# Cross-attention over the top ten rows: the first query projection in 32-column tiles, four side by side, in place of 64-column pairs

## The chip, the cores and the metric

The kernel runs on one core of one Trainium2 chip. The metric is the device time of one execution in microseconds (us). The kernel before took 146.26 us, the median of three runs (146.04 to 146.67). Instructions, waits and transfers are read from one profiled execution, taken by the hardware profiler.

## The reference

There are 8 batches. `x` is 8 x 224 x 512, the context is 8 x 750 x 512, all float32. For each batch:

```
scores   = x @ score_w + score_b                    # one number per row of x
topk_idx = top_k(scores, 10)
sparse   = x[topk_idx]                              # 10 rows of 512
q = sparse @ Wq.T + bq      (16 heads of 32)
k = ctx @ Wk.T + bk ;  v = ctx @ Wv.T + bv
attn = softmax(q k^T / sqrt(32))                    # 16 heads, 10 x 750
out  = (attn @ v) @ out_w.T + out_b
x[topk_idx] = out                                   # the other rows of x are returned as they came
```

The biases are eight times those first drawn. The output is all of `x` with ten rows per batch replaced.

## The kernel before, in words

Five engines run programs of their own, written out by hand, and wait for each other on semaphores. TensorE (PE) takes its matmuls in the order of the program at L762 to L794; nothing is reordered around a wait. The batches are worked in two groups: group 0 is batches 0 and 1, group 1 is batches 2 to 7 (`GROUPS`, L33). Group 0 is started as early as possible, so that TensorE has attention work while the rest of `x` is still arriving and being scored.

**The start, group 0.** SyncE (L191 to L200) queues, with no waits in between, two batches of `x`, Wq, one batch of `x`, Wk, two batches of `x`, the context columns of batch 0, the last three batches of `x`, the columns of batch 1 and the context rows of batches 0 and 1. A batch of `x` is 512 KB in memory. VectorE (DVE) scores each batch as it lands (two `tensor_tensor_reduce` per batch, L350), finds the top ten rows of group 0 (L366 to L378), and TensorE picks and transposes these 20 rows with small matmuls (`pick_rows` L590, `join_rows` L600) into `picked_T[0]`, which ScalarE copies out of PSUM (L275). `keep_warm` (L561) fills some of TensorE's waits with matmuls that nobody reads.

**The query projection, `project_queries(g)` (L620 to L635).** It computes Wq times the picked rows. The 512 outputs are four blocks `e` of 128, the 512 inputs four blocks `t` of 128. For each `e` and `t` the 128 outputs are cut into tiles of `TILE` = 64 columns of weights; the two tiles write to PSUM partitions 0 to 63 and 64 to 127, so they lie side by side in the array. Group 0 has 20 columns of moving data (2 batches x 10 rows), group 1 has 60. Each group has 4 x 4 x 2 = 32 calls. Each float32 call shows in the trace as two weight loads and two matmul records, so a group has 64 of each. Blocks `e` = 0 and 1 are the first half and end with one increment of `q_ps`, blocks 2 and 3 the second half with another.

**What takes the queries.** `spread_queries` on VectorE (L399 to L413) waits for each half, adds the bias (L405), spreads the result by head (L409) and increments `q_done`. VectorE has score work ahead of it and behind it: after both halves come the second product of batch 3, batch 4, a maximum over the key-bias terms (`copy_key_dot`, L434, which waits for four ScalarE copies at L297), and then batches 5, 6 and 7 (L527 to L532). `fold_keys` on TensorE (L637 to L650) waits for `q_done` 1, multiplies the first half by the key weights for all four steps, waits for `q_done` 2 and does the second half: 64 records each way, 80 columns wide. Then come `dot_key_bias(0)` (L677), in four tiles of 32 columns, and the logits of batch 0, `logits_by_step` (L700), 24 calls per batch and 48 records.

**The meeting point.** Ahead of the 21st of those 24 calls stands `transpose_scores(1)` (L575, placed by L778). It waits until VectorE has scored all eight batches and added the score bias (L363), and gives VectorE the scores of group 1 to choose from. TensorE takes nothing behind it before that. Four calls of batch 0 follow, then eight of batch 1 up to `move_idx` (L608). VectorE then chooses the rows of group 1, and turns to the softmax of batches 0 and 1.

**Afterwards** the batches follow each other: logits (L700, L714), softmax on VectorE and ScalarE, weighted sums of the context (`weigh`, L731). `project_queries(1)` lies inside the weighing of batch 1 (L782). SyncE loads further context when the logits of an earlier batch are done (L203 on). At the end come the value projection (`project_values`, L746, 32-column tiles, four side by side, 80 columns of moving data), the output projection (L758), and a scatter of 80 rows by GpSimd (L259).

Of the kernel before, what the change touches and what calls it, by code (L numbers as in the profile page):

```python
# [22 lines left out]
HEADS, TOPK = 16, 10  # L23
DH = D // HEADS
P = 128
# [19 lines left out]
FIRST = GROUPS[0][1]  # L45
PART = 32
TILE = 64
EARLY_COPIES = 5


def build(nc, x, x_lines, ctx_rows, ctx_cols, wq, wk, wv, wo, in_bias, out_b, score_row, out):
# [5 lines left out]
    with stack:  # L57
        def sb(name, shape, dt=F32):
            return stack.enter_context(nc.sbuf_tensor(name, shape, dt))
# [9 lines left out]
        wq_sb = sb("wq_sb", [P, DT, D])  # L69
# [31 lines left out]
        picked_T = [sb(f"picked_T{g}", [P, DT, b1 * TOPK]) for g, (b0, b1) in enumerate(GROUPS)]  # L101
# [35 lines left out]
        query_ps = [[logits_ps[1][:, 0, :], logits_ps[1][:, 1, :]], [logits_ps[0][:, 1, :], logits_ps[0][:, 0, :]]]  # L137
# [34 lines left out]
        def _(sp):  # L172
# [8 lines left out]
            def load_rows(b, n):  # L181
                sp.dma_start(ctx_r[n][:, :, :], ctx_rows[b, :, :, :]).then_inc(ctx_r_in[n], 16)
# [5 lines left out]
            def copy_x(b):  # L188
                sp.dma_start(out_pairs[:, b, :, :], x_sb[0:X_P, b, :, :]).then_inc(x_copied, 16)
# [22 lines left out]
            sp.dma_start(wo_sb[:, :, :], wo).then_inc(wo_in, 16)  # L212
            for b in range(EARLY_COPIES):
                copy_x(b)
            sp.wait_ge(logits_done, 3)
            load_cols(4, 0)
            for b in range(5, B):
# [3 lines left out]
                load_rows(b - 1, (b - 1) % 2)  # L221
                copy_x(EARLY_COPIES + b - 5)
            sp.wait_ge(mix_ready[1], B - 2)
# [334 lines left out]
        def _(pe):  # L558
# [36 lines left out]
            def join_rows():  # L595
                pe.wait_ge(regroup_done, 2 * FIRST + 1)
                pe.wait_ge(parts_done, 2)
                for t in range(DT):
                    for j in range(P // TILE):
                        last = nc.tensor.matmul(picked_ps[0][j * TILE:(j + 1) * TILE, t * FIRST * TOPK:(t + 1) * FIRST * TOPK],  # L600
                                                parts[:, t * P + j * TILE:t * P + (j + 1) * TILE],
                                                regroup[:, :, :].rearrange("p b q -> p (b q)"), start=True, stop=True)
# [17 lines left out]
            def project_queries(g):  # L620
                b0, b1 = GROUPS[g]
                nq = (b1 - b0) * TOPK
                if g:
                    pe.wait_ge(idx_ready, 1)
                pe.wait_ge(picked_T_done, g + 1)
                for half in range(2):
                    for k in range(2):
                        e = 2 * half + k
                        for t in range(DT):
                            for j in range(P // TILE):  # L630
                                c = e * P + j * TILE
                                last = nc.tensor.matmul(query_ps[g][half][j * TILE:(j + 1) * TILE, k * nq:(k + 1) * nq],  # L632
                                                        wq_sb[:, t, c:c + TILE], picked_T[g][:, t, b0 * TOPK:b1 * TOPK],
                                                        start=(t == 0), stop=(t == DT - 1), skip_group_check=True)
                    last.then_inc(q_ps, 1)  # L635

# [135 lines left out]
            join_rows()  # L772
            pe.wait_ge(wq_in, 16)
            project_queries(0)
            pe.wait_ge(wk_in, 16)
            fold_keys()
# [3 lines left out]
            logits_by_step(1, 1, [], {8: move_idx})  # L780
            weigh(0, 0, {})
            weigh(1, 1, {12: transpose_picked, 18: lambda: project_queries(1)})  # L782
            fold_pairs()
            dot_key_bias(1)
# [48 lines left out]
```

## Time and profile before

| what | value |
|---|---|
| median of three runs | 146.26 us (146.04 to 146.67) |
| the profiled execution, its own device time | 146.49 us |
| its span in the profile, first to last record | 144.3 us |
| TensorE (PE) busy | 136.3 us, 94% |
| TensorE weight loads (PEld) busy | 127.3 us, 88% |
| VectorE (DVE) busy | 81.8 us, 57% |
| first query projection, L632, group 0 | starts at 14.13 us, 64 records |
| `transpose_scores(1)`, L575 | starts at 25.64 us |

2.19 us of the device time lie outside the span. Times of single instructions are taken from the span's start. "PE" rows are matmuls, whose ends are modelled, so their durations overlap; the distance from one start to the next tells how fast they go. That distance is worked out from a merged row: (length of the row - mean duration of one) / (count - 1). "Idle before" in brackets is how long the engine had been idle ahead of a row, and for what.

### The profile page before, as it was taken

The page shows a single profiled execution, that of the slowest core. Times are in us where ns is not written, and L with a number is a line of the kernel's source. Part 1 is how long each engine was busy: PE and PEld are TensorE (multiplying, and loading weights), DVE is VectorE, ACT ScalarE, POOL GpSimd, SP SyncE. Part 2 cuts the span into 40 slices and gives each one's busy share as a digit, 9 for nine tenths or more (in the row PEclk, how much of TensorE's full clock was granted, in tenths as well). Part 3 has the DMA queues.
Part 4 walks back from the last instruction along what each step waited for, and adds up shares of the span by engine and source line. Part 5 has one row for each costly group of instructions (what it writes and reads, how often), then busy time and mean ns, then how long its engine had stood idle before and what let it go on. Part 6 is the DMA issues. An engine that isn't in the chain of part 4 may idle for free.

```text
span 144.3 us, 2951 instructions
## 1 busy us (share of the span) xinstructions
PE 136.3 (94%) x1262; PEld 127.3 (88%) x1262; DVE 81.8 (57%) x214; ACT 23.1 (16%) x48; POOL 4.7 (3%) x24
## 2 busy tenths in 40 slices
PE   7997997899999999999999999999999999999980
PEld 5544996898999998999999999999999999998840
DVE  2977658887880559088871575087138506735330
ACT  3001050003412051003140041005002300411100
POOL 6000000030000000000000000000000000000002
PEclk9999999999999999999999999999999999999997
DMA  4999999999988079999989884995880390000001
GB/s 157 395 409 418 422 409 360 433 429 379 407 269 371 7 252 420 326 395 398 427 320 313 297 356 119 343 302 235 269 294 0 49 392 0 0 5 0 5 0 45
DMA packets 5726, 37.61 MB, mean 261 GB/s; under 512 B 801, under 2 KB 801, under 8 KB 3410
## 3 DMA queue, kind: packets, MB, share of 16 engines
q1 hardware_dynamic: 5344, 36.93, 67.6%
q0 software_dynamic: 128, 0.33, 0.7%
q8 instruction: 10, 0.16, 0.5%
q10 hardware_dynamic: 242, 0.17, 0.5%
q14 instruction: 2, 0.02, 0.0%
HBM read 33.60 MB, written 3.83 MB: 259 GB/s over the span
## 4 chain that ended last, share of the span: by engine, by line
PE 76%; DMA 12%; SPq 4%; DVE 3%; issue 1%; POOLq 1%; ACT 1%; DVEq 0%
PE mix_ps L731 37%; PE logits_ps L714 23%; DMA x_sb<-x_lines_dram 12%; PE logits_ps L700 7%; PE logits_ps L758 3%; SPq L186 2%; PE logits_ps L666 2%; PE logits_ps L632 1%; PE mix_ps L666 1%; DVE product L350 1%; PE misc_ps L746 1%; ACT probs L306 1%; POOLq L57 1%; PE logits_ps L746 1%; SPq L179 1%
## 5 line engine op out<-in xcount | busy, mean ns | idle before, releaser
L731 PE MATMUL mix_ps<-probs,ctx_r 125*128 125x160 f32 x384 | 54.0, 300 | 0.2 <-ACT probs L306 0.2
L731 PEld LDWEIGHTS mix_ps<-probs,ctx_r 125*128 125x128 f32 x384 | 52.5, 190 | 1.0 <-issue 0.9
L714 PE MATMUL logits_ps<-qk,ctx_c 128*125 128x160 f32 x240 | 33.4, 299 | 0.0
L714 PEld LDWEIGHTS logits_ps<-qk,ctx_c 128*125 128x125 f32 x240 | 32.9, 188 | 0.0
L444 DVE TENSOR_REDUCE col_max<-logits_ps 125x160 f32<-125x960 f32 x8 | 9.2, 1154 | 25.7 <-PE logits_ps L714 21.3
L700 PE MATMUL logits_ps<-qk,ctx_c 128*125 128x160 f32 x144 | 20.5, 301 | 0.0
L700 PEld LDWEIGHTS logits_ps<-qk,ctx_c 128*125 128x125 f32 x144 | 19.6, 188 | 0.5 <-issue 0.4
L310 ACT ACTIVATE mix<-mix_ps 128x320 f32<-128x320 f32 x16 | 7.0, 440 | 64.5 <-PE mix_ps L731 64.4
L482 DVE TENSOR_REDUCE prob_sum<-probs 125x160 f32<-125x960 f32 x8 | 14.6, 1836 | 4.0 <-ACT probs L306 4.0
L306 ACT ACTIVATE probs<-probs 125x480 f32<-125x480 f32 x16 | 9.3, 603 | 29.3 <-DVE probs L476 29.3
L350 DVE CUSTOM_DVE_ANT_0 product<-x_sb,score_w_sb 112x512 f32<-112x512 f32 x16 | 10.4, 688 | 1.1 <-DMA x_sb<-x_lines_dram 1.1
L476 DVE TENSOR_TENSOR probs<-logits_ps,shift 125x480 f32<-125x480 f32 x16 | 9.8, 652 | 0.3
L561 PE MATMUL logits_ps<-ones 128*128 128x256 f32 (+2 forms) x16 | 7.6, 615 | 1.1 <-DVE ones L507 1.1
L561 PEld LDWEIGHTS logits_ps<-ones 128*128 128x128 f32 x16 | 4.1, 284 | 3.8 <-issue 2.5
L259 POOL DMA_INDIRECT out_dram<-y_sb,row_idx x1 | 0.9, 922 | 110.1 <-DVE y_sb L504 110.1
L632 PE MATMUL logits_ps<-picked_T,wq_sb 128*64 128x20 f32 (+1 forms) x128 | 4.1, 218 | 0.4 <-ACT picked_T L275 0.4
L632 PEld LDWEIGHTS logits_ps<-picked_T,wq_sb 128*64 128x64 f32 x128 | 3.9, 138 | 0.7 <-issue 0.7
L466 DVE COPY head_shift<-head_shift 32x5 f32<-32x5 f32 x24 | 3.9, 163 | 0.8
L405 DVE TENSOR_TENSOR q_sb<-logits_ps,bias_sb 128x40 f32<-128x40 f32 (+1 forms) x4 | 1.0, 240 | 5.9 <-PE logits_ps L632 5.9
L454 DVE COPY quad_max<-quad_max 32x5 f32<-32x5 f32 x24 | 3.8, 160 | 0.8
L487 DVE RECIPROCAL inv_sum<-misc_ps 128x320 f32<-128x320 f32 x1 | 2.2, 2158 | 3.5 <-PE misc_ps L684 3.5
L758 PE MATMUL logits_ps<-wo_sb,o_T 128*80 128x256 f32 x16 | 3.7, 381 | 0.0
(97 smaller groups left out, 75.2 us busy)
## 6 DMA issues: line engine op xcount, KB each, us to landing
ctx_r<-ctx_rows_dram SPq DMA_DIRECT2D x8, 1536.0 KB, 7.0
ctx_c<-ctx_cols_dram SPq DMA_DIRECT2D x6, 1500.0 KB, 9.0
x_sb<-x_lines_dram SPq DMA_DIRECT2D x8, 512.0 KB, 10.9
out_dram<-x_sb SPq DMA_DIRECT2D x8, 448.0 KB, 12.4
ctx_c<-ctx_cols_dram SPq DMA_DIRECT2D x4, 750.0 KB, 16.5
wq_sb<-wq_dram SPq DMA_DIRECT2D x1, 1024.0 KB, 7.0
wk_sb<-wk_dram SPq DMA_DIRECT2D x1, 1024.0 KB, 9.8
wv_sb<-wv_dram SPq DMA_DIRECT2D x1, 1024.0 KB, 9.6
```

What stands on the lines that cost most here:

```text
L306: nc.scalar.activation(part, part, ACT.Exp, scale=SCALE).then_inc(exp_done, 1)
L310: nc.scalar.activation(mix[:, 2 * half:2 * half + 2, :, b * TOPK:(b + 1) * TOPK], mix_ps[half][:, 0:2 * HQ].rearrange("p (t h q) -> p t h ...
L350: nc.vector.tensor_tensor_reduce(out=products[j][:, :], in0=x_sb[0:X_P, b, j, :], in1=score_w_sb[:, :], scale=1.0, scalar=0.0, op0=ALU.mul ...
L444: nc.vector.tensor_reduce(col_max[0:S_P, :], tiles(n).rearrange("p k t c -> p c k t"), AX.XY, ALU.max)\
L476: nc.vector.tensor_tensor(probs[n][:, k * BANK_T:(k + 1) * BANK_T, :], tiles(n)[:, k, :, :], shift[0:S_P, :].unsqueeze(1).broadcast_to([S_ ...
L482: nc.vector.tensor_reduce(prob_sum[:, b, :], probs[n][:, :, :].rearrange("p t c -> p c t"), AX.X, ALU.add)\
L561: nc.tensor.matmul(logits_ps[1][:, 1, 0:n], ones[:, :], ones[:, 0:1].broadcast_to([P, n]), start=True, stop=True)
L632: last = nc.tensor.matmul(query_ps[g][half][j * TILE:(j + 1) * TILE, k * nq:(k + 1) * nq], wq_sb[:, t, c:c + TILE], picked_T[g][:, t, b0 * ...
L700: last = nc.tensor.matmul(logits_ps[n][0:S_P, t // BANK_T, (t % BANK_T) * HQ:(t % BANK_T + 1) * HQ], ctx_c[n][:, f, t, :], qk[:, b, f, :], ...
L714: last = nc.tensor.matmul(logits_ps[n][0:S_P, t // BANK_T, (t % BANK_T) * HQ:(t % BANK_T + 1) * HQ], ctx_c[n][:, f, t, :], qk[:, b, f, :], ...
L731: last = nc.tensor.matmul(mix_ps[half][:, f * HQ:(f + 1) * HQ], ctx_r[n][0:S_P, t, c:c + P], probs[n][:, t, :], start=(t == 0), stop=(t == ...
L758: last = nc.tensor.matmul(logits_ps[0][0:BQ, half, 0:D // 2], o_T[:, e, :], wo_sb[:, e, cols], start=(e == 0), stop=(e == DT - 1))
```

## The change

A constant `FIRST_TILE` = 32 is added. `project_queries(0)` cuts each block of 128 outputs into four tiles of 32 columns of weights, which write to PSUM partitions 0, 32, 64 and 96 on, in place of two tiles of 64. `project_queries(1)` keeps `TILE` = 64. The calls of group 0 go from 32 to 64; the moving data stays 20 columns, the waits and increments and where results lie stay as they are.

```diff
@@ -45,6 +45,7 @@
 FIRST = GROUPS[0][1]
 PART = 32
 TILE = 64
+FIRST_TILE = 32
 EARLY_COPIES = 5
@@ -620,6 +621,7 @@
             def project_queries(g):
                 b0, b1 = GROUPS[g]
                 nq = (b1 - b0) * TOPK
+                tile = TILE if g else FIRST_TILE
                 if g:
                     pe.wait_ge(idx_ready, 1)
                 pe.wait_ge(picked_T_done, g + 1)
@@ -627,10 +629,10 @@
                     for k in range(2):
                         e = 2 * half + k
                         for t in range(DT):
-                            for j in range(P // TILE):
-                                c = e * P + j * TILE
-                                last = nc.tensor.matmul(query_ps[g][half][j * TILE:(j + 1) * TILE, k * nq:(k + 1) * nq],
-                                                        wq_sb[:, t, c:c + TILE], picked_T[g][:, t, b0 * TOPK:b1 * TOPK],
+                            for j in range(P // tile):
+                                c = e * P + j * tile
+                                last = nc.tensor.matmul(query_ps[g][half][j * tile:(j + 1) * tile, k * nq:(k + 1) * nq],
+                                                        wq_sb[:, t, c:c + tile], picked_T[g][:, t, b0 * TOPK:b1 * TOPK],
                                                         start=(t == 0), stop=(t == DT - 1), skip_group_check=True)
                     last.then_inc(q_ps, 1)
```

## Rows read from the trace of the kernel before

**Rows 1.** The page, part 1: busy us (share of the span) xinstructions, by engine.
```profile
span 144.3 us, 2951 instructions
PE 136.3 (94%) x1262; PEld 127.3 (88%) x1262; DVE 81.8 (57%) x214; ACT 23.1 (16%) x48; POOL 4.7 (3%) x24
```

**Rows 2.** Chain of waits in time, 6 to 26 us: start us, us, what.
```profile
6.39 17.59 DMA x_sb<-x_lines_dram
...
24.00 0.69 DVE product L350
...
25.35 0.24 DVE biased_scores L363
...
25.64 0.35 PE misc_ps L575 x2
```

**Rows 3.** Timeline, 13.6 to 18.8 us: start us, us, engine, line, operation, forms, count.
```profile
14.13 2.05 PE L632 MATMUL logits_ps<-picked_T,wq_sb 128*64 128x20 f32 x64 [0.42 <-ACT picked_T L275]
...
15.35 0.20 DVE L405 TENSOR_TENSOR q_sb<-logits_ps,bias_sb 128x40 f32<-128x40 f32 x1 [0.84 <-PE logits_ps L632]
15.58 0.32 DVE L409 TENSOR_TENSOR q_diag<-q_sb,head_mask 128x160 f32<-128x160 f32 x1
16.05 0.78 PE L645 MATMUL mix_ps<-q_diag,wk_sb 128*64 128x80 f32 x16
...
16.45 0.32 DVE L409 TENSOR_TENSOR q_diag<-q_sb,head_mask 128x160 f32<-128x160 f32 x1
...
17.18 0.75 PE L645 MATMUL mix_ps<-q_diag,wk_sb 128*64 128x80 f32 x16
...
18.42 0.16 PEld L677 LDWEIGHTS logits_ps<-q_diag,key_rep 128*32 128x32 f32 x8
```

**Rows 4.** Timeline, 46 to 48.5 us, PE: the second query projection.
```profile
46.25 2.08 PE L632 MATMUL logits_ps<-picked_T,wq_sb 128*64 128x60 f32 x64
```

**Rows 5.** Timeline, 133.9 to 136.5 us, PE: value projection, two of its rows.
```profile
134.25 0.74 PE L746 MATMUL logits_ps<-mix,wv_sb 128*32 128x80 f32 x32
134.80 0.74 PE L746 MATMUL misc_ps<-mix,wv_sb 128*32 128x80 f32 x32
```

**Rows 6.** Lines L632, L677: duration ns min/median/max, first and last start us.
```profile
L632 PE MATMUL logits_ps<-picked_T,wq_sb x64: 204/213/233, 14.1 to 16.0; 128*64 128x20 f32 x64
L632 PE MATMUL logits_ps<-picked_T,wq_sb x64: 222/222/267, 46.3 to 48.1; 128*64 128x60 f32 x64
L677 PEld LDWEIGHTS logits_ps<-q_diag,key_rep x8: 106/108/109, 18.4 to 18.5; 128*32 128x32 f32 x8
```

**Rows 7.** Timeline, 18.8 to 26 us, up to the meeting point.
```profile
18.69 5.70 PE L700 MATMUL logits_ps<-qk,ctx_c 128*125 128x160 f32 x40
18.84 0.34 ACTq L318 DMA_DIRECT2D out_b_sb<-out_b_dram  x1
...
19.99 0.50 DVE L434 TRANSPOSE_TENSOR_REDUCE key_dot<-key_rows 32x10 f32<-32x320 f32 x1 [1.39 <-ACT key_rows L297]
20.91 0.69 DVE L350 CUSTOM_DVE_ANT_0 product<-x_sb,score_w_sb 112x512 f32<-112x512 f32 x1 [0.42 <-DMA x_sb<-x_lines_dram]
...
24.00 0.69 DVE L350 CUSTOM_DVE_ANT_0 product<-x_sb,score_w_sb 112x512 f32<-112x512 f32 x1 [0.51 <-DMA x_sb<-x_lines_dram]
...
25.64 0.35 PE L575 MATMUL misc_ps<-ident,biased_scores 112*6 112x112 f32 x2 [1.24 <-DVE biased_scores L363]
```

**Rows 8.** Line L186, the loads of x: issues, and time to landing.
```profile
L186 SPq DMA_DIRECT2D x_sb<-x_lines_dram x8: 371/434/635, 0.8 to 6.4; - x8
DMA to landing us min/median/max: 3.3/10.9/17.6
```

**Rows 9.** DMA issues: KB, median us from issue to landing.
```profile
out_b_sb<-out_b_dram ACTq DMA_DIRECT2D x1, 160.0 KB, 7.8
```

**Rows 10.** Windows, PE: length, busy us (x), granted clock (PEclk), DMA share, GB/s.
```profile
140.10:142.30 2.20, 0.00 (x0) 1.00 0.00 0
142.30:144.30 2.00, 0.00 (x0) 0.51 0.28 82
```

## The prediction

> **What bounds the kernel now.** The first part of the page shows a kernel held by TensorE: 136.3 of 144.3 us busy [rows 1]. That is the average. The change touches one stretch, from 14.13 us on, and what a gain there is worth depends on who is late next. So the chain of waits comes second. The reader is to see that from 6.39 to 24.00 us it does not run over TensorE at all: it is the load of the last batch of x, then VectorE's products of it, its scores with the bias at 25.35, and only then TensorE's transpose at L575, at 25.64 [rows 2]. The third view is the timeline up to that transpose. TensorE has run out of the 20 logits calls ahead of it at 24.39 (18.69 + 5.70) and stands idle for 1.24 us, until VectorE's scores are there; VectorE in turn stood idle for 0.51 us until the last x landed [rows 7]. That x was issued at about 6.4 us and landed 17.6 us later [rows 8]; SyncE waits for nothing that the projection produces before it. Whatever TensorE wins between 14.13 and 24.39 us therefore ends as a longer idle time at 25.64.
>
> **The change, part by part.** All sums are against the profiled execution: span 144.3 us, device time 146.49 us, which is 0.23 above the median of 146.26.
>
> *The block itself.* Now 64 records start within 2.05 - 0.213 = 1.84 us, 29.2 ns apart [rows 3, 6]. In the second projection the moving data is three times as wide (60 columns for 20) and 64 records take (2.08 - 0.222)/63 = 29.5 ns each [rows 4, 6]. The pace does not follow the moving columns, so it is set by the weight loads of 64 columns. Afterwards there are 128 records, with 32-column loads. No row shows 32-column tiles with 20 moving columns. The fast end: in the key-bias product eight loads of 32 columns start within 0.16 - 0.108 = 0.05 us, 7.4 ns apart [rows 3, 6]; 128 x 7.4 = 0.95 us. That is also what half the columns at the same rate gives (29.2 / 4 = 7.3 ns per record). The next row is the value projection, same tile width but 80 moving columns: 32 records in 0.55 us, 17.2 ns each [rows 5], so 2.20 us. The slow end: a record costs what one costs in this block now, 128 x 29.2 = 3.74 us. I take 0.95: the value projection streams four times as many columns, and here the loads are the limit. The block gets shorter by 1.87 - 0.95 = 0.92 us; between the ends, from 0.92 shorter to 1.87 longer.
>
> *A rule that speaks against it.* The trace's own fastest run of many matmul records is 17.2 ns from start to start [rows 5]. The Trainium skill, page "TensorE: Matmul & The Clock Gate", section "Wait — 56ns, not 53.3ns?", says that start to start never falls below about 25 ns however few columns stream. By that rule the block would take 128 x 25 = 3.2 us, an estimate, 1.33 us longer than now, and the kernel would end some 0.4 us later. The trace disagrees: the value projection's 17.2 ns are already below it.
>
> *What waits for it, first half.* The last record of the half starts 31 x 29.2 ns after 14.13, at 15.04; VectorE begins at 15.35 and has spread the half at 15.90 (15.58 + 0.32); TensorE's key fold begins at 16.05 [rows 3]. With 7.4 ns the last of 64 records starts at 14.60, 0.44 us earlier, and so does each of the others: spread by 15.46, fold from 15.61. VectorE is free for it: it has waited 0.84 us before L405 [rows 3].
>
> *Second half.* TensorE has issued it by 15.07 and then has to wait about 0.3 us for VectorE, an idle time that is new: half of the block's gain ends here. VectorE takes the second half right behind the first, two operations, 0.56 us with the gap between them (16.21 to 16.77 now) [rows 3], so to about 16.05. The fold needs it after its first 32 records, 1.13 us (16.05 to 17.18) [rows 3], at 16.74. No wait. The change of tile width between projection and fold lies inside the new idle time, and that ahead of the projection in the idle time before it (0.42 us) [rows 3]: nothing.
>
> *Up to the meeting point.* Fold, key-bias product and the first logits move forward by 0.44 us; TensorE is done at 23.95 instead of 24.39. The transpose at L575 stays at 25.64, because the last x still lands at 23.98 (6.4 + 17.6) [rows 8] and VectorE needs the same 1.6 us for it. TensorE's idle time grows from 1.24 to 1.68 us. VectorE's L434 starts 0.44 earlier too, and then waits 0.86 instead of 0.42 us for x [rows 7]. Cost and gain: 0.
>
> *What moves with it.* ScalarE's load of the output bias, 160 KB, is issued behind its copies at 18.84 and takes 7.8 us [rows 7, 9]. Issued 0.44 us earlier, some 0.44/7.8 x 160 = 9 KB more of it go ahead of the last x. Between no effect and a last x that lands later by the whole 0.44 us by which the load moves, I take 0.02 us: 9 KB are little beside the loads of x alone, eight of 512 KB each by 23.98 us [rows 8]. SyncE's next loads wait for the logits of batch 0, which come behind L575: unmoved.
>
> Sum: -0.44 at the fold, +0.44 at L575, +0.0 to 0.02 for the load: 146.49 + 0.0, and against the median 146.3 us.
>
> **The rivals.**
> *A, the gain comes through.* Were x not late, or had TensorE the longer way to 25.64, the 0.44 us would be kept: 145.8 us. For it speaks only that TensorE is busy 94% of the span [rows 1]; against it the 1.24 us of idle time at L575 and VectorE's own waits for x [rows 7]. x would have to land over 1.2 us earlier than in the profiled execution. The most that could be kept, if the second half's gain came through as well, is 0.92: 145.3 us.
>
> *B, a call costs what it costs now, and there are twice as many.* Then the block takes 3.74 us, 1.87 more, by the same count of records at 29.2 ns. TensorE's spare 1.24 us would go, but VectorE's is smaller and decides: its L434 waits for ScalarE, which waits for TensorE, and behind L434 the waits for x leave 0.42 + 0.51 = 0.93 us [rows 7]. A delay up to 0.93 us, or 21.9 ns per record (1.87 + 0.93 = 2.80 us over 128), costs nothing; beyond it each us costs one. 1.87 - 0.93 = +0.94: 147.2 us. For it: twice as many instructions have to be fed to TensorE, and the only row at 7.4 ns has eight of them [rows 6]. Against it: 17.2 ns over 128 records in the value projection, which by itself (block 2.20 us, +0.33) stays inside the 0.93.
>
> *C, the clock.* The longer idle time could cost TensorE its full clock. The trace has the clock at full until 142.3 us although TensorE did nothing from 140.1 on, and at half after that [rows 10]: 2.2 us of idleness did not lower it, and 1.68 is less. If it fell all the same, the logits behind L575 would run at half speed (1.2 for 2.4 GHz): 24 records up to the next other work (4 calls of batch 0, 8 of batch 1), at 5.70/40 = 0.14 us each [rows 7], so up to 3.4 us more, 149.7 us.
>
> **How the numbers follow.** Forecast (no change in the end) 88%, A 6%, B 4%, C 2%. A difference of under 0.5%, 0.73 us, can't be told from none. The forecast lies within it; A at 0.44 does too, and passes it only with nearly all of the block's 0.92 us, 2%. B and C are beyond it, 6% together, of which a part of B (delays between 0.93 and 1.66 us) would stay inside: 5% slower. So 2% faster, 93% within, 5% slower. The range: A's 145.8 at the low end; at the high end the runs shown (up to 146.67) and the milder half of B, 146.8 us.
>
> **What would show it.** In the changed kernel's profile: 128 records at the projection's line with starts some 7 to 8 ns apart (B: 22 or more); L405 at about 14.9 and fold from about 15.6; a new idle time of TensorE ahead of the fold; L575 still at 25.6, with 1.7 us of idle time instead of 1.24; every stage after 26 us at its old time. I am wrong if L575 moves by more than 0.2 us in either direction, or if the span changes though L575 stands still.

## The result, and the profile after

The changed kernel takes 149.81 us, the median of four runs (149.34 to 150.66), against 146.31 us (146.04 to 146.67) for the kernel before in the same comparison: ratio 1.0253, 95% interval 1.0224 to 1.0283. It is 2.5% slower. The forecast was no change, 146.3 us within 145.8 to 146.8. The profiled execution took 149.34 us with a span of 147.2 us, 2.9 us more than before. Now and then an execution of any of these kernels, the kernel before included, runs several us longer at a lower granted clock; all ratios and run times below leave those out.

Parts 1 and 3 of the page after (queues: packets, MB, share of 16 DMA engines); the q8 line reads the same before:

```profile
span 147.2 us, 3079 instructions
PE 136.6 (93%) x1326; PEld 127.8 (87%) x1326; DVE 81.5 (55%) x214; ACT 23.1 (16%) x48; POOL 4.8 (3%) x24
...
q8 instruction: 10, 0.16, 0.5%
```

The busy time of TensorE has hardly moved (136.3 to 136.6 us). What is new is time in which it does nothing. The timeline of the changed kernel, in the stretch of [rows 3]:

```profile
13.92 1.29 PE L634 MATMUL logits_ps<-picked_T,wq_sb 128*32 128x20 f32 x128 [0.42 <-ACT picked_T L276]
14.78 0.20 DVE L406 TENSOR_TENSOR q_sb<-logits_ps,bias_sb 128x40 f32<-128x40 f32 x1 [0.58 <-PE logits_ps L634]
...
15.48 0.78 PE L647 MATMUL mix_ps<-q_diag,wk_sb 128*64 128x80 f32 x16 [0.27 <-DVE q_diag L410]
15.50 0.32 DVE L410 TENSOR_TENSOR q_diag<-q_sb,head_mask 128x160 f32<-128x160 f32 x1
...
16.05 0.75 PE L647 MATMUL misc_ps<-q_diag,wk_sb 128*64 128x80 f32 x16
...
16.61 0.23 PE L647 MATMUL mix_ps<-q_diag,wk_sb 128*64 128x80 f32 x1
...
19.85 0.70 PE L647 MATMUL mix_ps<-q_diag,wk_sb 128*64 128x80 f32 x14 [3.01 <-issue]
...
21.12 0.50 PE L679 MATMUL logits_ps<-q_diag,key_rep 128*32 128x80 f32 x8
```

The projection does nearly what was forecast: 128 records in 1.29 us, 8.7 ns apart, and the fold begins 0.57 us earlier (0.21 of it because this execution reached the projection earlier). Then, one matmul into the second half of the fold, TensorE stands for 3.01 us. VectorE had delivered the second half at 15.82 us (15.50 + 0.32), and the row names no engine and no transfer: "issue" means that nothing in the profile accounts for the wait.

The second loss follows from the first. Windows of the changed kernel (columns as in [rows 10]) and its timeline up to L576 (L575 before), where [rows 7] had 5.70 us for the same 40 records and 1.24 us of idle time:

```profile
14.00:21.00 7.00, 3.72 (x192) 1.00 1.03 418
21.00:24.50 3.50, 3.50 (x23) 0.51 1.02 413
24.50:28.60 4.10, 4.10 (x33) 1.00 1.03 379
```

```profile
21.55 7.11 PE L702 MATMUL logits_ps<-qk,ctx_c 128*125 128x160 f32 x40
28.49 0.36 PE L576 MATMUL misc_ps<-ident,biased_scores 112*6 112x112 f32 x2
```

TensorE stands without work from 16.84 to 19.85 us and goes on at full clock; at 21.0 us the granted clock falls to half (1.2 GHz), and it is back at full (2.4 GHz) from 24.5 us. The balance at L576 against [rows 3] and [rows 7]: fold begins 0.57 earlier (16.05 to 15.48); from there to the first logits 6.07 us against 2.64, so 3.43 later, of which 3.01 are the stop; the 40 records 1.41 us longer; the two rows now overlap by 0.17 and the 1.24 us of idle time are used up: -0.57 + 3.43 + 1.41 - 0.17 - 1.24 = +2.86, and 28.49 - 25.64 = 2.85 (the last digit is rounding). Behind L576 every stage keeps its length: the span is 2.9 us longer.

### The profile page after: what moved, and what is told of

The parts are those of the page before. It is cut to its first block, busy times and chain, and to the rows that moved or that the text cites. A ratio compares the mean times of both kernels' runs of the same rounds, so it can differ in the third digit from the quotient of the medians.

```text
span 147.2 us, 3079 instructions
## 1 busy us (share of the span) xinstructions
PE 136.6 (93%) x1326; PEld 127.8 (87%) x1326; DVE 81.5 (55%) x214; ACT 23.1 (16%) x48; POOL 4.8 (3%) x24
## 4 chain that ended last, share of the span: by engine, by line
PE 88%; DVE 5%; issue 4%; ACT 1%; POOLq 1%; DVEq 0%
PE mix_ps L733 36%; PE logits_ps L716 22%; PE logits_ps L702 12%; PE logits_ps L562 3%; PE logits_ps L760 2%; PE logits_ps L634 2%; PE logits_ps L668 1%; PE mix_ps L668 1%; PE mix_ps L647 1%; PE misc_ps L748 1%; ACT probs L307 1%; POOLq L58 1%; PE misc_ps L647 1%; PE mix_ps L569 1%; PE logits_ps L591 1%
## 5 line engine op out<-in xcount | busy, mean ns | idle before, releaser
L716 PE MATMUL logits_ps<-qk,ctx_c 128*125 128x160 f32 x240 | 33.4, 299 | 0.0
L716 PEld LDWEIGHTS logits_ps<-qk,ctx_c 128*125 128x125 f32 x240 | 32.9, 188 | 0.0
L702 PE MATMUL logits_ps<-qk,ctx_c 128*125 128x160 f32 x144 | 21.9, 314 | 0.0
L702 PEld LDWEIGHTS logits_ps<-qk,ctx_c 128*125 128x125 f32 x144 | 21.1, 199 | 0.6 <-issue 0.6
L562 PE MATMUL logits_ps<-ones 128*128 128x256 f32 (+2 forms) x16 | 7.0, 573 | 1.1 <-DVE ones L508 1.1
L647 PE MATMUL mix_ps<-q_diag,wk_sb 128*64 128x80 f32 x32 | 1.8, 236 | 3.3 <-issue 3.0
L435 DVE TRANSPOSE_TENSOR_REDUCE key_dot<-key_rows 32x10 f32<-32x320 f32 (+1 forms) x2 | 1.7, 833 | 5.1 <-ACT key_rows L298 5.0
L647 PEld LDWEIGHTS mix_ps<-q_diag,wk_sb 128*64 128x64 f32 x32 | 1.5, 136 | 3.4 <-issue 3.4
L406 DVE TENSOR_TENSOR q_sb<-logits_ps,bias_sb 128x40 f32<-128x40 f32 (+1 forms) x4 | 1.0, 242 | 5.3 <-PE logits_ps L634 5.3
```

Of the source, the lines that this page charges most:

```text
L562: nc.tensor.matmul(logits_ps[1][:, 1, 0:n], ones[:, :], ones[:, 0:1].broadcast_to([P, n]), start=True, stop=True)
L647: last = nc.tensor.matmul(fold_ps[step][j * TILE:(j + 1) * TILE, e * w:(e + 1) * w], wk_sb[:, e, c:c + TILE], q_diag[0][:, e, :, :, :].rea ...
L702: last = nc.tensor.matmul(logits_ps[n][0:S_P, t // BANK_T, (t % BANK_T) * HQ:(t % BANK_T + 1) * HQ], ctx_c[n][:, f, t, :], qk[:, b, f, :], ...
L716: last = nc.tensor.matmul(logits_ps[n][0:S_P, t // BANK_T, (t % BANK_T) * HQ:(t % BANK_T + 1) * HQ], ctx_c[n][:, f, t, :], qk[:, b, f, :], ...
```

## The experiments

**Theory S, instruction supply.** TensorE's program is brought to it while it runs. In what follows a step is one recorded instruction of TensorE: a weight load, a matmul or a semaphore operation. The stop comes behind step 449. The page counts packets of code on queue q8, 16 KB each: the eight profiles with 2562 to 2690 steps (before and after among them) have 10 of them, the five with 2778 to 2846 steps have 11, so q8 brings TensorE's program, and 2562 to 2690 steps over 10 packets are some 256 to 269 per packet. The projection now has 128 more such steps (64 loads, 64 matmuls), and its steps pass more than three times as fast (8.7 ns per matmul record for 29.2). TensorE reaches the end of the code that it has before the next packet is there. The kernel before reaches step 449 only at 21.92 us; its first packet starts at 17.82, and it does not stop. In the changed kernel the stop begins before the packet does. DMA view of the changed kernel for q8, 17.4 to 18.7 us (in 16.3 to 17.4 us there is no such row):

```profile
q8 instruction: 1, 0.02, 5.3%
```

The record of the packet starts at 17.50 and takes 1.1 us; the stop lasts from 16.84 to 19.85.

**Theory T.** The narrow tiles do it: their pace, or the change from 32 to 64 columns behind them.

**1. The wide projection, with as many instructions as the narrow one.**

```diff
+            def fill(calls):
+                for i in range(calls):
+                    j = i % 4
+                    nc.tensor.matmul(logits_ps[0][j * PART:(j + 1) * PART, 0, 0:FIRST * TOPK], ones[:, 0:PART],
+                                     ones[:, 0:FIRST * TOPK], start=True, stop=True, skip_group_check=True)
...
             project_queries(0)
+            fill(32)
```

This is the kernel before, with its 64-column projection. A call of `fill` has 32 columns of ones as weights and 20 moving columns, and nobody reads its result.

> The kernel before, with its 64-column projection, and 32 small matmul calls (32 columns of ones, 20 moving columns, results unread, 64 records, 128 instructions) right behind the first query projection. Theory S, instruction supply: TensorE's code arrives in packets of 16 KB, and in the changed kernel TensorE had used up what was there at 16.84 us, after 450 of its records, and stood until 19.85. Here the same place in the instruction stream (450 records) is reached at about 17.6 us, while the packet comes no earlier: an idle time of about 2.2 us, put down to nothing, in the fold, and with 0.5 us of filler and 1.2 us of spare time at L575 about 1 to 2.5 us slower than before (147.3 to 148.8 us). Theory T, the narrow projection itself (its pace or the change from 32 to 64 columns behind it) stops TensorE: no long idle time, at most 0.5 us later at the fold, all of it hidden at L575, 146.3 us.

149.38 us (148.44 to 149.92), ratio 1.023, interval 1.0174 to 1.0285; 147.3 to 148.8 was expected. Timeline of TensorE and windows:

```profile
14.10 2.05 PE L638 MATMUL logits_ps<-picked_T,wq_sb 128*64 128x20 f32 x64 [0.42 <-ACT picked_T L275]
16.08 0.74 PE L567 MATMUL logits_ps<-ones 128*32 128x20 f32 x64
...
17.91 0.23 PE L651 MATMUL mix_ps<-q_diag,wk_sb 128*64 128x80 f32 x1
20.29 0.70 PE L651 MATMUL mix_ps<-q_diag,wk_sb 128*64 128x80 f32 x14 [2.14 <-issue]
```

```profile
0.00:19.00 19.00, 10.98 (x222) 1.00 0.92 365
...
22.00:24.00 2.00, 2.00 (x16) 1.00 1.04 422
```

The projection is the old one, and the stop is there, at the same instruction of the fold and as long as expected (2.14 us). The first window counts weight loads: 222 until the stop (the changed kernel: 222 until 18 us as well), and in both it is step 449. The fillers are narrow themselves, so this run alone does not clear narrow tiles as such; the runs of part 2 do. In this profiled execution, the fastest of the four (148.44 us), the clock stayed at full after the stop, and its span is still 2.0 us longer than that of the kernel before. The other three took 148.86 to 149.92 us at a lower mean granted clock (0.977 to 0.988 against 0.995), so part of the 2.3% is probably the clock.

**2. More instructions, but early.** Forty small calls in the warm-up, at 5.8 us, in place of one call of 512 columns and ahead of the narrow projection.

```diff
-            keep_warm(WARM_SCORES)
+            keep_warm(WARM_SCORES[1:])
+            fill(40)
```

`WARM_SCORES` is (512, 256, 128) columns; the second run has `fill(24)`.

> The changed kernel with one 512-column warm-up call at 4.2 us replaced by 40 small calls (80 records), so that TensorE has more instructions, not fewer, but most of the added ones early. Theory S: the boundary after which the next packet is asked for is crossed by about 8 us instead of 14, the packet is there before the projection; the boundary after that falls into the first logits, at about 20 us, some 5.3 us after its request: idle time under 0.6 us, total 146.1 to 146.6 us. Theory T: the narrow projection is unchanged, the idle time of 3 us stays, 149.5 us. The count of calls is a guess to within some ten.

146.90 us, ratio 1.004, interval 0.9991 to 1.009; 146.1 to 146.6 was expected. The 3 us are gone although TensorE has 156 steps more than the changed kernel. The start became slower: the 512-, 256- and 256-column calls from 7.97 us on took 3.64 us against 2.51 in the kernel before, the projection began at 15.05 us, and the granted clock was at half from 15.1 to 18.5 us.

> As the run with 40 calls, with 24. Theory S: the request moves only to about 13 us and the boundary falls into the projection itself, at about 15 us: an idle time of 2 to 3.5 us inside the projection instead of in the fold, 148.5 to 150 us. Theory T: 3 us between the same two instructions of the fold as in the changed kernel.

153.81 us, ratio 1.0521, interval 1.0479 to 1.0562. Timeline of TensorE:

```profile
16.48 1.80 PE L640 MATMUL logits_ps<-picked_T,wq_sb 128*32 128x20 f32 x116 [0.43 <-ACT picked_T L276]
22.33 0.41 PE L640 MATMUL logits_ps<-picked_T,wq_sb 128*32 128x20 f32 x12 [4.06 <-issue]
22.67 1.34 PE L653 MATMUL mix_ps<-q_diag,wk_sb 128*64 128x80 f32 x16
23.79 1.28 PE L653 MATMUL misc_ps<-q_diag,wk_sb 128*64 128x80 f32 x16
```

Here the stop lies inside the projection, between two equal calls, where nothing changes width. Before it lie 106 matmuls and 116 more: 222 again. The time missed its expectation (148.5 to 150 us), and the stop (2 to 3.5 us) too. Not all of the 5.2% is the stop: the fold's first 16 records take 1.12 us (22.67 to 23.79), where [rows 3] has 0.58, which is the pace of half clock (the profile's first record of the clock, at full, is at 26.2 us), and the steps of the projection are slower than the changed kernel's as well. What the two runs compare cleanly is the place of the stop, not the total.

**3. The packet without other traffic.**

```diff
-            load_x(3, 5)
+            load_x(3, 4)
+            sp.wait_ge(q_ps, 2)
+            load_x(4, 5)
             load_cols_by_half(0)
```

> The changed kernel, with SyncE waiting for the end of the first projection (q_ps 2) before it issues the loads of x from batch 4 on and all context. The data queues are empty from about 13.7 to 15.2 us. The total gets longer by the wait (x comes some 2 us later), it is the idle time at the fold that counts. Theory S with transfers that hold the packet up: the packet is asked for at about 14.3 us and lands by about 16, no idle time of TensorE in the fold. If the packet's way is long by itself, about 3 us of idle time stay. Theory T: 3 us stay.

152.28 us in a single execution (x comes late, as intended). TensorE's timeline, and q8 in the window from 15.2 to 16.3 us:

```profile
16.61 0.23 PE L649 MATMUL mix_ps<-q_diag,wk_sb 128*64 128x80 f32 x1
17.57 0.64 PE L649 MATMUL mix_ps<-q_diag,wk_sb 128*64 128x80 f32 x13 [0.73 <-issue]
```

```profile
q8 instruction: 1, 0.02, 5.4%
```

Up to the stop this execution is the changed kernel's to within 0.01 us. The packet starts at 15.29 instead of 17.50, and TensorE goes on at 17.57 instead of 19.85. Both are 2.2 to 2.3 us earlier, so 2.2 us of the packet's delay came from the full data queues. This is one execution, but in all others the packet starts 2.7 us or more after TensorE passes step 193, which lies 256 ahead of the stop, and here 1.1 us (more on this step in the next section). The stop does not vanish, against my number: from the packet's start to the next instruction 2.3 us pass here too (2.35 in the changed kernel, 2.37 to 2.55 at the first stop of the four others that have one).

**4. The narrow projection with its code in time and the clock kept.** Forty calls of 64 moving columns in place of the 512- and the 128-column one.

> As the run with 40 early calls, but the calls are 64 columns wide and stand for the 512- and the 128-column warm-up call, so that TensorE is as busy as before until 7.5 us. Theory S: no stop of TensorE in projection or fold, projection at 14 us as in the kernel before, its 128 records in about 1.3 us, L575 at 25.6; 146.0 to 146.5 us, the same as before within 0.5%. Rival: part of the 2.5% belongs to something else in the narrow projection; then at least 0.5% remains.

146.12 us, ratio 0.9991, interval 0.9972 to 1.0009. Timeline:

```profile
14.10 1.29 PE L640 MATMUL logits_ps<-picked_T,wq_sb 128*32 128x20 f32 x128 [0.42 <-ACT picked_T L276]
14.63 0.69 DVE L351 CUSTOM_DVE_ANT_0 product<-x_sb,score_w_sb 112x512 f32<-112x512 f32 x1 [1.13 <-DMA x_sb<-x_lines_dram]
...
16.08 0.78 PE L653 MATMUL mix_ps<-q_diag,wk_sb 128*64 128x80 f32 x16 [0.69 <-DVE q_diag L410]
...
21.29 3.96 PE L708 MATMUL logits_ps<-qk,ctx_c 128*125 128x160 f32 x28 [0.68 <-issue]
25.30 0.35 PE L582 MATMUL misc_ps<-ident,biased_scores 112*6 112x112 f32 x2
```

This is the run that separates the parts: the same 128 narrow records, and no loss. The total that was forecast for the change is there once the code is in time. A smaller stop (0.68 us) now comes behind step 705, which is 256 on from 449, and is hidden ahead of L582. But the fold begins no earlier than in the kernel before (16.08), because VectorE waits 1.13 us for batch 3 of x, which it scores ahead of the queries. So the run does not show an earlier fold being swallowed at the transpose; and as the kernel before was not run with these forty early calls, what they alone cost or gain is not known.

**5. Half of the change, and fewer instructions behind it.**

```diff
-                tile = TILE if g else FIRST_TILE
...
                 for half in range(2):
+                    tile = TILE if g or half else FIRST_TILE
```

> Only the first half of the projection in 32-column tiles (32 + 16 calls, 64 instructions more than before instead of 128). Theory S: TensorE again stops behind its 450th record, which now lies just behind the fold, at about 18 us, and goes on at about 19.9: idle 1.9 us, of which 0.9 at least are hidden by VectorE's waits for x: 146.5 to 147.5 us. A rival by which the stop comes with the change from 32 to 64 columns: a stop ahead of or in the fold, as long as in the changed kernel.

147.27 us, ratio 1.0061, interval 1.0038 to 1.0084. Timeline and window:

```profile
17.88 0.26 PE L679 MATMUL logits_ps<-q_diag,key_rep 128*32 128x80 f32 x1
20.09 0.34 PE L679 MATMUL logits_ps<-q_diag,key_rep 128*32 128x80 f32 x7 [1.96 <-issue]
20.36 7.38 PE L702 MATMUL logits_ps<-qk,ctx_c 128*125 128x160 f32 x40
```

```profile
22.00:24.00 2.00, 2.00 (x9) 0.50 1.02 408
```

With 64 steps fewer the stop sits 64 steps further on in the program, again behind step 449. It is as long as expected (1.96 us), and the total is where it was expected. In this profiled execution the clock fell after it, where in run 1 it stayed up after 2.14 us. It is the slowest of the four, 148.42 us at a mean granted clock of 0.988; the others took 146.79 to 147.34 us at 0.994 to 1.000. The stop alone costs little here, and the clock probably did not fall in each execution of one and the same kernel.

```diff
-                            for j in range(P // TILE):
+                            for j in range(1):
```

This is `fold_keys` of the changed kernel, one call of 128 columns where it had two of 64.

> The changed kernel with the key fold in one 128-column call where it had two of 64 (32 calls become 16, 64 instructions fewer; the stream of 80 columns sets its pace either way). Theory S: TensorE stops behind record 450 again, which now lies at the end of the fold or in the key-bias product, at about 17.8 us, and goes on at about 19.9: idle about 2 us in place of 3; with the idle time partly hidden and the clock lowered or not, 146.8 to 148.5 us. Rival by which the change of tile width behind the projection matters: the stop stays where it was, at the second half of the fold.

147.89 us (147.26 to 149.12), ratio 1.0092, interval 1.0059 to 1.0126. Timeline and window:

```profile
15.63 1.09 PE L647 MATMUL mix_ps<-q_diag,wk_sb 128*128 128x80 f32 x8 [0.27 <-DVE q_diag L410]
16.55 1.06 PE L647 MATMUL misc_ps<-q_diag,wk_sb 128*128 128x80 f32 x8
...
20.79 0.34 PE L679 MATMUL logits_ps<-q_diag,key_rep 128*32 128x80 f32 x7 [1.21 <-issue]
```

```profile
21.60:25.00 3.40, 3.40 (x15) 0.50 1.05 424
```

The stop moved behind the fold, as S says, and is shorter than expected (1.21 us for 2). Even behind these 1.21 us the clock fell, at 21.6 us. My premise was wrong: 8 records take 0.92 us, 115 ns each, against some 70 ns for a pair of 64-column ones (1.13 us for 16 pairs, [rows 3]), so the fold takes 3.7 instead of 2.4 us. The moving data do not set this pace, since the same 80 columns pass a pair of tiles in 70 ns. That points to the 128-column load; no run takes it apart further.

**6. What binds at L575.** Another order at the meeting point.

```diff
+            add_score_bias(1)
+            find_max(0, 0)
+            find_shift(0)
+            subtract_max(0, 0)
             choose_eight(1)
             choose_rest(1)
-            find_max(0, 0)
+            find_max(1, 1)
...
-            logits_by_step(0, 0, [qk_done], {20: lambda: transpose_scores(1)})
+            logits_by_step(0, 0, [qk_done], {})
             pe.wait_ge(key_rows_done, DT)
-            logits_by_step(1, 1, [], {8: move_idx})
-            weigh(0, 0, {})
-            weigh(1, 1, {12: transpose_picked, 18: lambda: project_queries(1)})
+            logits_by_step(1, 1, [], {2: lambda: transpose_scores(1)})
+            weigh(0, 0, {6: move_idx})
+            weigh(1, 1, {14: transpose_picked, 19: lambda: project_queries(1)})
```

VectorE does the softmax of batch 0 before it chooses the rows of group 1. TensorE transposes the scores within batch 1, and `move_idx` and the two insertions into the weighing of batch 1 come later.

> The kernel before, its projection 64 columns wide, with another order at the meeting point: TensorE transposes the scores of group 1 three calls into batch 1 instead of four before the end of batch 0, and VectorE does the softmax of batch 0 before it chooses the rows of group 1. If the last x and VectorE's order, and not TensorE, set the time from 24 to 34.35 us, as the prediction said, the weighing of batch 0 starts at about 32.5 instead of 34.35 us and the whole is 1.3 to 1.9 us shorter, 144.4 to 145 us. If TensorE's own work sets it, 146.3.

145.57 us, ratio 0.9951, interval 0.9935 to 0.9968: faster, but by 0.7 us instead of 1.3 to 1.9. Repeated:

> The new order at the meeting point alone, as before, for comparison on the same chip: 0.5% less than the kernel before.

145.50 us, ratio 0.9951, interval 0.9933 to 0.9968. TensorE's timeline in the kernel before, and in this run:

```profile
34.35 10.02 PE L731 MATMUL mix_ps<-probs,ctx_r 125*128 125x160 f32 x72 [0.17 <-ACT probs L306]
```

```profile
26.12 0.78 PE L706 MATMUL logits_ps<-qk,ctx_c 128*125 128x160 f32 x4 [0.67 <-DMA ctx_c<-ctx_cols_dram]
...
32.92 1.80 PE L737 MATMUL mix_ps<-probs,ctx_r 125*128 125x160 f32 x12
```

The weighing starts 1.43 us earlier than the 34.35 of the kernel before, with a new wait of 0.67 us for the context columns of batch 1. At the end 0.9 us are left (span 143.4 against 144.3). Most of the rest is no loss: `move_idx`, four small calls, stood ahead of the weighing in the kernel before (29.19 us) and lies in it now, 0.37 us from its start to the next row:

```profile
34.64 0.44 PE L614 MATMUL misc_ps<-ones,idx_diag 2*80 2x1 f32 x4
```

> Both: the new order at the meeting point, the narrow projection, and the 40 early calls of 64 columns that bring the code in time. With the spare time at L575 gone, the 0.4 us that the narrow projection saves ahead of the fold should now reach the end: 0.2 to 0.4 us less than the new order alone. Rival: x still ends the wait at L575 and nothing comes of it.

145.67 us, ratio 0.9966, interval 0.9946 to 0.9987: nothing gained over the order alone, against the 0.2 to 0.4 us that I expected. TensorE's timeline:

```profile
14.73 1.29 PE L646 MATMUL logits_ps<-picked_T,wq_sb 128*32 128x20 f32 x128 [0.42 <-ACT picked_T L276]
16.28 0.77 PE L659 MATMUL mix_ps<-q_diag,wk_sb 128*64 128x80 f32 x16 [0.27 <-DVE q_diag L415]
...
21.39 5.65 PE L714 MATMUL logits_ps<-qk,ctx_c 128*125 128x160 f32 x40 [0.57 <-issue]
```

The fold does begin 0.37 us earlier relative to the projection than in [rows 3] (1.55 us behind it instead of 1.92), and TensorE stands for 0.57 us at the next code boundary, again behind step 705.

> New order, narrow projection, 40 early calls of 64 columns, and the fold in 128-column calls. In the run without the last part TensorE stopped for 0.57 us behind record 706, early in the first logits, at 21.4 us: the packet asked for at record 450, inside the projection, was not there. With 64 instructions fewer in the fold record 706 comes some 4 us later and Theory S expects no stop at all. Then 0.4 us of the narrow projection should reach the end: 0.2 to 0.5 us less than the new order alone, and faster than both kernels. If not, what the narrow projection saves is lost elsewhere.

146.02 us, ratio 0.9988, interval 0.9964 to 1.0011. No stop any more, but the fold in 128-column calls costs 1.4 us (first logits at 20.08 us against 18.66 with the order alone), so the run settles nothing about the narrow projection, and its expectation failed. The lowest times are those of the new order with the old projection (145.57 and 145.50 us); its ratio's interval overlaps that of the new order with the narrow one.

## Why the prediction was wrong

*Where the end is set.* Right as far as it was tested. The last x and VectorE's scores held L575 at 25.64 [rows 7]; the new order of run 6, which takes TensorE's wait for them away, gains 0.7 us; and with the code in time the kernel with the narrow projection takes as long as the one before: 0.9991 (run 4). My sum also has the earlier fold end as idle time at L575; no run shows that, since in run 4 the fold was not earlier.

*The block.* Right in mechanism, short in size: 128 records in 1.29 us, 8.7 ns apart where I took 7.4. The 7.4 was read off weight loads (the row at L677 is a PEld row); the matmuls of the same eight calls are some 16 ns apart on average, so the row did not support it as firmly as I wrote. The rule of 25 ns from start to start (the Trainium skill, page "TensorE: Matmul & The Clock Gate", section "Wait — 56ns, not 53.3ns?") does not hold for column tiles side by side: the trace has a third of it.

*What waits for it.* The first half came out as worked out: L406 0.86 us behind the projection's start, against 1.22 before [rows 3], the fold 1.56 against 1.92.

*The second half and the fold, "No wait".* This is the step that failed. I priced 64 added calls by their time in the array and by nothing else. I asked who waits for whom in the program, and did not ask whether the program itself arrives. The page of the profile shows that it does not come for nothing: 10 packets on q8, spread over the run, on the same DMA engines that are busy without a break meanwhile (DMA share 1.02 from 16 to 24 us of the kernel before). From the projection's start to the fold's end TensorE has 256 load and matmul steps in 4.3 us before the change [rows 3], and 384 in 3.9 us by my own sum for after it, where the logits have 2 in 0.14 us. What the runs showed in its place: TensorE stood 3.01 us in the second half of the fold for its own code. Runs 1 and 2 show it: the stop follows the count (step 449, 221 or 222 loads) and not the tiles.

*Rival B* had the right form (more instructions than can be fed) and the wrong measure: I bounded it by the pace of the records, and the records ran at full pace until they ended.

*Rival C* was priced for an idle time of 1.68 us. The real one was 3.01, and the clock did fall; half clock cost 1.41 us on the logits and part of the 0.42 beside the stop in the stretch before. What I had argued from [rows 10], that 2.2 us of idleness do not lower the clock, was a poor reading to begin with: the clock did fall at 142.3 us, with TensorE idle since 140.1. It also fails on the runs: the clock fell after 1.96 us in one execution of the half-narrow kernel and after 1.21 us in the run with the wide fold; after 2.14 us in run 1's profiled execution it did not. The length of the idle time alone does not decide.

*The range* left out every cost that was not in the program. TensorE reached L575's place 4.1 us later (-0.57 + 3.43 + 1.41 - 0.17), 3.3 times the 1.24 us that it had to spare there.

*When the packet is asked for* no record shows. The counts suggest that it is one packet ahead, when TensorE passes step 449 - 256 = 193. The changed kernel passes it at 14.19 us, the kernel before at 15.08. The first packet starts 3.3 and 2.7 us later, 2.7 to 4.8 us later in all runs with full data queues, and 1.1 us later in run 3; where early calls brought step 193 forward to 7.6 to 8.6 us, the packet came at 11.4 to 11.9. On this reading the 3.01 us are 14.19 + 3.31 (until the packet starts) + 2.35 (until the next instruction) - 16.84.

What stays open: the 2.3 to 2.6 us between the packet's start and the next instruction, of which its record covers 1.1; what decides whether the clock falls after a stop; and what the early calls cost by themselves.

## What to carry to other kernels

Splitting calls into narrower tiles multiplies instructions. Where calls pass in some 10 ns, count instructions per microsecond and compare with the code packets on the page: in this kernel, with the data queues full, the 256 steps ahead of a stop and the stop together took 5.7 us (changed kernel) and 6.5 us (run 4). A dense burst, one engine's idle time put down to "issue" and an instruction queue that has to share full DMA engines belong together; adding instructions early can cure what adding them late has caused (run 4), if TensorE's clock is kept up meanwhile (run 2).

## What the runs showed of the hardware that was not expected

- TensorE stopped behind the same step, its 449th recorded instruction (221 or 222 weight loads), in six kernels with different programs ahead of it: in the fold, in the projection, in the key-bias product. Two more kernels stopped behind step 705. The kernel before passes step 449 at 21.92 us, 4.1 us behind its packet's start, without a stop. The Trainium skill, page "Runtime: NRT & Kernel Launch", section "Instruction fetch mechanics", says that code comes in blocks of 16 KiB, 256 instructions, and that the fetch is hidden because instructions are issued more slowly than blocks arrive. The size agrees (0.16 MB in 10 packets, stops 256 steps apart); that it is hidden does not: 0.57 to 4.06 us were open.
- The first packet's record lasts 0.96 to 1.11 us. In the four runs where it came at 11.4 to 11.9 us, batch 3 of x landed at 14.5 to 14.7 us; in the nine others, the run with 24 early calls and a packet at 20.0 among them, at 13.1 to 13.7. So code that is fetched early may take back part of what it wins, as at the fold of run 4; that the packet delays the batch was not tested by itself.
- 40 early calls of 20 columns let TensorE come later to the projection (15.05 us), 40 of 64 columns did not (14.10 us, as before). The start also varies by itself: in the first run of part 6, whose TensorE program is the old one up to there, the projection began at 15.03 us.
